# A graph network of four layers on one core: broadcasts ahead of a flag, weight loads sooner, and a sum of two cells moved into TensorE's turning

## The reference, cut to what matters

```python
def _gru_cell(x, hstate, Wih, Whh, bih, bhh):
    gi = x @ Wih.T + bih
    gh = hstate @ Whh.T + bhh
    ...
    r = sigmoid(ir + hr); z = sigmoid(iz + hz)
    n = tanh(inn + r * hn)
    return (1.0 - z) * n + z * hstate

def _gat_head(h, node_adj, edge_adj, W, a):
    hW = h @ W
    ...
    att = where(edge_adj > 0, e_plus[None, :], NEG_INF)
    att = where(edge_adj < 0, e_minus[None, :], att)
    att = softmax(att, axis=1)
    return att * edge_adj @ hW

edge_output = _gru_cell(node_support, h, edge_Wih, ...)
edge_support = (sum of the three heads) / 3
node_output = _gru_cell(edge_support, h, node_Wih, ...)
return de[:, None] * edge_output + dn[:, None] * node_output   # de, dn: the diagonal of adj, one vector here
```

## Time and profile before

| | us |
|---|---|
| runs without a profile: median of 3 (2772.74 to 2773.79) | 2773.63 |
| profiled execution, its own time | 2772.22 |
| its span, first to last instruction | 2770.6 |
| PE busy, share of the span | 80% |
| DVE | 71% |
| ACT | 54% |
| POOL | 6% |
| mean granted TensorE clock, share of 2.4 GHz | 0.893 |

### The profile page before, as it was taken

How to read it: one execution, slowest core, us unless ns; L and a number is a source line. 1 busy time by engine, 2 the same in 40 slices (tenths; PEclk the granted TensorE clock), 3 DMA queues, 4 the chain that set the end, 5 groups by cost and what they waited for, 6 DMA issues and landing times.

```text
span 2770.6 us, 18272 instructions
## 1 busy us (share of the span) xinstructions
PE 2208.5 (80%) x5974; PEld 958.7 (35%) x5974; DVE 1967.4 (71%) x2267; ACT 1500.9 (54%) x1508; POOL 174.5 (6%) x289
## 2 busy tenths in 40 slices
PE   6664555565599999999998399960299989999997
PEld 3221222222244444444443244430133324444443
DVE  8887999999799888888968644679999993000000
ACT  3006999999877777777757623330388883000000
POOL 1001111121110000000000000012100000000000
PEclk9666778778799999999999699985699999999999
DMA  9999888989754333333330088967566657988994
GB/s 337 387 389 356 311 343 348 351 346 391 292 188 152 117 124 126 114 123 123 111 122 0 1 314 275 327 246 264 184 228 216 207 197 246 307 298 300 306 312 141
DMA packets 189358, 659.47 MB, mean 238 GB/s; under 512 B 13968, under 2 KB 26736, under 8 KB 145872
## 3 DMA queue, kind: packets, MB, share of 16 engines
q1 hardware_dynamic: 161408, 551.89, 57.3%
q0 software_dynamic: 27856, 106.43, 10.1%
HBM read 611.92 MB, written 46.33 MB: 238 GB/s over the span
## 4 chain that ended last, share of the span: by engine, by line
PE 60%; DVE 21%; issue 6%; SPq 5%; DMA 4%; ACT 3%; POOL 0%; DVEq 0%; POOLq 0%; ACTq 0%
PE bank L662 24%; PE bank L845 16%; DVE arena L1548 12%; PE bank L751 8%; PE bank L799 7%; SPq L283 5%; DMA arena<-in_adj 2%; PE bank L804 2%; PE bank L639 1%; DVE arena L1529 1%; DVE arena L1872 1%; DMA arena<-in_adjT 1%; DVE arena L1818 1%; DVE arena L1289 1%; DMA mask_d<-arena 1%
## 5 line engine op out<-in xcount | busy, mean ns | idle before, releaser
L662 PE MATMUL bank<-arena 128*128 128x512 f32 x1536 | 661.3, 593 | 15.0 <-DVE arena L1611 15.0
L1548 DVE CUSTOM_DVE_ANT_0 arena<-arena 128x2048 f32<-128x2048 bf16 x192 | 435.6, 2318 | 14.5 <-DVE arena L1548 7.8
L845 PE MATMUL bank<-arena 128*128 128x512 f32 x1024 | 442.0, 592 | 0.3 <-ACT arena L1175 0.3
L1611 DVE TENSOR_TENSOR arena<-arena 128x2048 f32<-128x2048 f32 x192 | 433.2, 2283 | 3.4 <-ACT arena L1032 2.0
L662 PEld LDWEIGHTS bank<-arena 128*128 128x128 f32 x1536 | 292.3, 190 | 383.6 <-issue 383.6
L990 ACT ACTIVATE arena<-arena 128x2048 f32<-128x2048 f32 x192 | 384.0, 2000 | 31.1 <-DVE arena L1548 16.4
L639 PE MATMUL bank<-arena 128*128 128x512 f32 x512 | 273.9, 693 | 126.0 <-ACT arena L971 112.4
L1023 ACT ACTIVATE arena<-arena 128x2048 f32<-128x2048 f32 x128 | 244.4, 1911 | 151.0 <-DVE arena L1600 150.9
L1887 DVE TENSOR_TENSOR arena<-arena,bank 128x512 f32<-128x512 f32 x8 | 5.3, 685 | 418.7 <-PE bank L819 418.7
L845 PEld LDWEIGHTS bank<-arena 128*128 128x128 f32 x1024 | 193.4, 190 | 238.3 <-issue 237.7
L799 PE MATMUL bank<-arena 128*128 128x512 f32 x512 | 238.7, 609 | 24.0 <-DVE arena L1872 23.9
(11 more groups left out here) (255 smaller groups left out, 2135.2 us busy)
## 6 DMA issues: line engine op xcount, KB each, us to landing
arena<-in_adjT SPq DMA_DIRECT2D x384, 1024.0 KB, 6.7
arena<-in_adj SPq DMA_DIRECT2D x128, 1024.0 KB, 5.2
mask_d<-arena POOLq DMA_DIRECT2D x64, 512.0 KB, 7.3
arena<-mask_d POOLq DMA_DIRECT2D x64, 512.0 KB, 5.6
arena<-hw_d SPq DMA_DIRECT2D x64, 192.0 KB, 2.3
arena<-e_d POOLq DMA_DIRECT2D x6, 1024.0 KB, 11.2
hw_d<-hw_c POOLq DMA_DIRECT2D x32, 192.0 KB, 5.9
arena<-nm_d POOLq DMA_DIRECT2D x6, 1024.0 KB, 10.2
```

Source lines behind the costliest of these rows:

```text
L662: last = pe.matmul(banks[B * half + b][:], hw_ring[n % HRING][:, h * C:(h + 1) * C], probs[k % 4][:, b * CH:(b + 1) * CH], start=(t == 0 a ...
L845: last = pe.matmul(banks[spec_banks[half][b]][:], stationary[:, t, :], ring[slot][:, b * CH:(b + 1) * CH], start=(t == 0), stop=(t == T - 1))
L1548: v.tensor_tensor_reduce(logits[k % 3], mask, e_row, FAR_UNIT, FAR, ALU.add, ALU.min, NMF[:, col:col + 1])\
L1611: v.tensor_tensor(probs[k % 4], probs[k % 4], ring[k // HEADS % HRING], ALU.mult)\
```

## The change

Three edits. (1) The first three broadcasts are issued ahead of the wait for the flag and its reading, each with its own semaphore (`first_row_loaded`); DVE waits for each ahead of that head's first use, where it waited for all ahead of its first step. (2) SP loads the first five pieces of hW after the first five stores and the last maximum; the wait for all 32 stores stands behind them. (3) Cell 1's last two DVE steps go: DVE leaves z's product with the difference in `step_1`, ACT writes the tanh to `new_1`, and PE makes the sum while it turns: for each of four blocks, three accumulating matmuls (with the identity, the identity, and half of it) stand for one transpose. `step_1` and `new_1` are double; DVE and ACT wait for the turning two blocks earlier. DVE makes `half_ident` once, ahead of the maxima.

```diff
+        half_ident = sb("half_ident", [P, P])
...
                         if n == HRING - 1:
+                            sp.wait_ge(S["hw_stored"], 16 * HRING)
                             sp.wait_ge(S["logits_ready"], 2 * T * HEADS)
-                            sp.wait_ge(S["hw_stored"], 16 * T)
                             for early in range(HRING):
                                 load_weights(early)
+                            sp.wait_ge(S["hw_stored"], 16 * T)
...
             pool.wait_ge(S["edges_stored"], 32)
-            pool.wait_ge(S["flag_ready"], 1)
-            any_negative = pool.value_load(flag_i[NEG0:NEG0 + 1, 0:1], min_val=0, max_val=1)
...
-            broadcast(0, 0, 0, "e_broadcast")
+            for h in range(HEADS):
+                pool.dma_start(e_bc[:, h, :], e_d[h, 0:HALF].partition_broadcast(P)).then_inc(first_row_loaded[h], 16)
+            pool.wait_ge(S["flag_ready"], 1)
+            any_negative = pool.value_load(flag_i[NEG0:NEG0 + 1, 0:1], min_val=0, max_val=1)
             with pool.If(any_negative):
...
                 for b in range(B):
-                    last = pe.transpose(banks[3][:, b * P:(b + 1) * P], so[q % 2][:, b * P:(b + 1) * P], ident[:])
+                    cols = slice(b * P, (b + 1) * P)
+                    pe.matmul(banks[3][:, cols], so[q % 2][:, cols], ident[:], start=True, stop=False)
+                    pe.matmul(banks[3][:, cols], new_1[q % 2][:, cols], ident[:], start=False, stop=False)
+                    last = pe.matmul(banks[3][:, cols], step_1[q % 2][:, cols], half_ident[:], start=False, stop=True)
...
+                    if k == HEADS - 1:
+                        act.wait_ge(S["logits_used"], 2 * T * HEADS + 3)
...
+                    if cell == 1 and q >= 2:
+                        act.wait_ge(S["gru_turned"], q - 1)
-                    act.activation(gn[cell], gt[cell], ACT.Tanh, bias=bi[:, cell, 2:3]).then_inc(S["gate_n"], 1)
+                    act.activation(new_1[q % 2] if cell else gn[0], gt[cell], ACT.Tanh, bias=bi[:, cell, 2:3]).then_inc(S["gate_n"], 1)
...
+            ts(half_ident[:], ident[:], 0.5, None, ALU.mult)
...
-                    elif j == 0 and not signed and part < 2:
-                        dve.wait_ge(S["second_broadcast" if part else "e_broadcast"], 16 * HEADS)
+                    elif j == 0 and not signed and part == 1:
+                        dve.wait_ge(S["second_broadcast"], 16 * HEADS)
...
+                        if n == 0:
+                            dve.wait_ge(first_row_loaded[h], 16)
                         dve.wait_ge(S["logits_used"], k + 1)
...
-                    ch(v.scalar_tensor_tensor(t_, z, 1.0, t_, ALU.add, ALU.mult))
                     if cell == 0:
+                        ch(v.scalar_tensor_tensor(t_, z, 1.0, t_, ALU.add, ALU.mult))
...
                     else:
-                        ch(v.scalar_tensor_tensor(t_, t_, 0.5, h_new, ALU.mult, ALU.add))
-                        dve.wait_ge(S["gru_out"], n)
-                        v.tensor_tensor(so[q % 2], so[q % 2], t_, ALU.add).then_inc(S["gru_out"], 1)
+                        if q >= 2:
+                            dve.wait_ge(S["gru_turned"], q - 1)
+                        v.scalar_tensor_tensor(step_1[q % 2], z, 1.0, t_, ALU.add, ALU.mult).then_inc(S["gru_out"], 1)
```

More of the change, by code:

```diff
@@ L161, in build @@
         so = [at(R + 80 + 2 * i, CH) for i in range(2)]
+        step_1, new_1 = ([at(R + 88 + 4 * i + 2 * j, CH) for j in range(2)] for i in range(2))
         x_add = at(R + 84, CH)
@@ L245, in build @@
         heads_loaded = [sem(f"heads_loaded{i}") for i in range(HRING)]
+        first_row_loaded = [sem(f"first_row_loaded{h}") for h in range(HEADS)]
         x_loaded = [sem(f"x_loaded{i}") for i in range(4)]
@@ L1510, in maxima @@
                     if j == 0 and signed and part != 2:
-                        dve.wait_ge(S["e_broadcast"], 16 * HEADS * (part - part // 2 + 1))
+                        if part:
+                            dve.wait_ge(S["e_broadcast"], 16 * HEADS * (part - part // 2))
                         dve.wait_ge(S["second_broadcast"], 16 * HEADS * (part - part // 2 + 1))
-                    elif j == 0 and not signed and part < 2:
-                        dve.wait_ge(S["second_broadcast" if part else "e_broadcast"], 16 * HEADS)
+                    elif j == 0 and not signed and part == 1:
+                        dve.wait_ge(S["second_broadcast"], 16 * HEADS)
                     for m in (n, n + 1) if n % 2 == 0 else ():
@@ L1628, in _ @@
                     n, bank = 2 * q + cell, banks[4 * cell:4 * cell + 4]
-                    r, z, t_, h_new = gr[cell], gz[cell], gt[cell], gn[cell]
+                    r, z, t_, h_new = gr[cell], gz[cell], gt[cell], new_1[q % 2] if cell else gn[0]
                     dve.wait_ge(S["gate_r"], n + 1)
```

## The result

The kernel after takes 2769.00 us (median of 17 runs, 2766.80 to 2771.71), the kernel before in the same measurement 2774.15 (17 runs, 2769.91 to 2777.07). The ratio is 0.9985, 95% interval 0.9979 to 0.9991: between 2.5 and 5.8 us faster, 4.2 in the middle. The time lies in the range of the prediction, 2.6 above its single value. By the bound of 0.2% it is no change, where the prediction gave "faster" 0.70.

A forecast was written before the change was run, and what follows sets the result against it. Long TensorE or VectorE stages bound most of the kernel, and the change can win only at three joints: 3.5 + 2.2 + 1.5 = 7.2 us won, giving 2766.4 us for the runs, range 2760 to 2771.

The forecast's parts named there:

- faster: Whole kernel: a measured time below 2768.1 us, more than 0.2% (5.5 us) under before; chance 0.70.
- Joint 1: Edge values' store through first broadcast to VectorE's first maximum: tile 1 7.4 us sooner, 3.5 left after the mask store's wait.
- the bound of 1.5: Lower bound of the gain at the first broadcasts, in us, if the late sixth broadcast adds its 2.5 once more.
- The first maximum: VectorE's first maximum starts when the first broadcast lands, near 222.5 us, with clearing and mask done by 217.2.
- Joint 2: Last hW store through SP's load of piece 0 to the first head matmul: 2.2 us sooner, bounds 1.8 and 2.5.
- the 7.7 that I gave no place in the sum: At the hW pieces: us won if pieces land ahead of tile 4's end, out of order of issue.
- Joint 3: The cells: TensorE becomes the bound, block 13.2 us instead of 14.00; 4.8 won less 3.3 at the end, 1.5 net.
- the bare turning: The cells' last turning, after TensorE's idle time: mostly half clock, 4.8 us, 3.3 longer than before up to ACT's scaling.
- Rival B: First broadcasts: mask store lands at 245.7 or later and takes all their gain; 3.7 us won, 2769.9; chance 0.13.
- Rival A: First broadcasts: mask store lands before 240, so the 7.4 us stay; 11.1 won in all, 2762.5; chance 0.12.
- rival C: The cells: turning instructions take 0.22 us throughout, 5.3 a turning; kernel 9.2 us slower, 2782.8; chance 0.07.

The follow-up runs named there:

- SP held: The kernel after, with SP's load of tile 4 held until the first mask store has landed: ratio 0.9982 to the kernel before.
- e6_pieces_ahead: The kernel after, with the five pieces of hW issued ahead of the heads' tiles 3 and 4 on SP: 2761.36 us, ratio 0.9961 to before.
- e12_heads_branch_turned: e8_three_mended with VectorE's branch ahead of the heads turned round, the code that runs right behind it: 2753.95 us, ratio 0.9933 to before.
- e8_three_mended: The kernel after, with second three broadcasts at tile 4, hW pieces ahead of tiles 3 and 4, last cell block in old form: 2757.38 us, 0.9943.

## Why the prediction came out as it did

**Joint 1: the mechanism held, the term was too large.** That tile 1 gains much, that the mask's buffer takes it back, that SP's loads come sooner and share the engines: all is in the rows. But 3.5 became 0.8 in the first pair of profiles and 1.7 over all of them: from the store to the third mask step 32.81 to 34.42 in the five kernels that have the first edit as in the diff, with nothing else changed at this joint (mean 33.77), 35.07 to 36.10 in the four without (mean 35.46). That lies just inside the bound of 1.5. The failing step is the landing of the mask's store. I had it at 239.8 with nothing beside it and at 242.2 with SP's loads, which is 29.3 and 31.7 after the store's issue; measured were 30.77 (SP held) and 34.33. Two terms are short. The queue without SP's new loads is 1.5 slower: I moved all landings by the 1.25 of the earlier issue, and they did not move. After the store's issue the first broadcast lands at 13.2 (mean of the same five kernels; 13.4 in the four) and the third at 19.5 (19.3 in the four), although it is issued 1.0 sooner; in the profile of after the third takes 12.6 us where it took 10.20. The broadcasts leave while SP's earlier loads still fill the engines (share 1.00 at 218 to 219 us; the last of these loads lands 10.9 after the store in after, 10.7 in before), and I take that for the cause. And SP's loads cost 3.6 and not 2.4.

**The first maximum came 2.2 later than I said.** The first broadcast lands 6.7 after its issue, not 5.4, is issued 0.2 later than I said, and the maximum follows 0.8 behind the landing. I had clearing and mask done by 217.2 behind the transfer; they ended 0.5 behind the landing. Two things that I didn't foresee hold them back: VectorE's idle 5.65 at the branch, and the clearing, which takes 1.95 where two such steps took 0.49. Its first step runs beside POOL's own masking (223.57, 1.16 us long); in all seven kernels where the two overlap the clearing takes 1.36 to 2.19, in the others 0.49. Before, an idle time at the branch would lie unseen in the 14.26 us of waiting.

**Joint 2: right in mechanism, less than its lower bound.** 2.2 was said, with 1.8 as the least; the seven kernels with the edit as in the diff have 15.74 to 16.02 (mean 15.89), the four without 16.98 to 17.46 (mean 17.24): 1.35. In the pair of profiles the piece lands 1.05 behind tile 4 and not 0.5, and tile 4 itself takes 8.5 and not 7.9. The queue kept its order, as I took it, and the 7.7 that I gave no place in the sum needed another order: e6_pieces_ahead and e12_heads_branch_turned won 5.5 and 7.6 on top.

**Joint 3: twice the size, by what happens at the two ends.** Over the kernels that have the edit as in the diff the cells take 160.06 to 161.08 (mean of seven 160.60), without it 163.49 to 163.76 (mean of four 163.61): 3.0 won, 1.5 said. TensorE became the bound, with 2.68 for a turning (2.9 said) and 12.98 for a block (13.2 said). From the first to the seventh turning that is 3.9 (81.78 before, 77.88 after): five blocks win 1.08 each on average, 5.4 together, and the block between the first two turnings, which was TensorE's before too, grows from 11.49 to 12.98. That 1.5 I had put at nothing. The rest of the difference lies at the end. I charged the bare turning with 3.3; from the seventh turning to ACT's scaling it took 12.16 before and 13.05 after, 0.9 more. The turning itself is 3.6 longer, as I feared, but what I undervalued is that VectorE's two additions also go ahead of it, where TensorE is not the bound. The eighth turning starts 7.87 after the seventh instead of 10.56; 1.46 of that are the additions, and the other 1.2 I take for VectorE's lead over a TensorE that is now the bound.

**The sum.** 1.7 + 1.35 + 3.0 = 6.0 where 7.2 was said, and 4.2 (2.5 to 5.8) by the runs. That joint 1's lead "stays, down to the heads" is not shown: from the store to the end of the maxima the same five kernels take 538.7 on average (536.8 to 540.8), the four 539.3 (537.3 to 540.5). That is 0.5 sooner and not 1.7, within a spread that is larger than either; with 0.5 the sum would be 4.9. The heads give nothing back: 661.66 without and 661.76 with the edits, mean of four and of seven. Rival B's time, 2769.9, is the nearest, but not for B's reason: joint 1 gave something, and joint 3 made up for half of what the others lacked. That the time still lies in the stated range is in part owed to this: errors of opposite sign met. Rival A needed the mask's store before 240; rival C's price of 0.22 was paid only in the last turning. "Faster" did not come, because 4.2 us is under the 5.5 of 0.2% and the prediction's 7.2 was not far above it: 0.70 was too much where two of the three terms could, and did, come out near or under the lower ends of their bounds (1.7 with a bound of 1.5, 1.35 with 1.8).

## What to carry to other kernels

When an edit pulls a transfer forward, look up what follows it in the same queue and what its consumer then frees sooner: here the store behind six broadcasts, and the loads that a faster VectorE set off, took back most of the 4.9 us that were won. A transfer wanted first has to be issued first, ahead of the megabytes in its queue or in another queue; the order was worth 4.6 us for the store and 5.5 for the pieces, where broadcasts issued 1.0 us sooner into full engines landed no sooner. And a chain that shows an engine idle for nothing, right behind a branch, asks for the code that runs to be put directly behind that branch; at the one branch where this was tried it won 2.0 us.

## What the runs showed of the hardware that I had not expected

VectorE stood idle for nothing, where it jumps to the second part of a branch, 5.5 to 5.7 us ahead of the maxima in every kernel with the broadcasts ahead of the flag, and 3.6 ahead of the heads once the pieces came early enough; with the heads' code in place, that one was gone. The second idle time was on the chain of e6_pieces_ahead and e8_three_mended, the first on that of after, where the mask's store could only be issued behind it.

The identical kernel needs 501.9 or 505.1 us for the same 62 half rows of maxima, from one execution to the next: the difference is that of its waits of 0.7 to 3.5 us for tile loads and a mask store, the first of them 64 to 66 us apart (328, 394 and 458 us in before).

A clearing step of VectorE, 128 by 128 words, took 1.75 us where POOL's own masking (L447) ran beside it, and 0.29 in e8_three_mended, where it did not.
